# Four inverse roots per pair of tiles from GpSimd to VectorE, the share transposes inside their own pair, scatters unpaced

## The chip, the cores and the metric

One core of a Trainium2 chip runs the whole program. The metric is the device time of one launch in microseconds (us). The engines are TensorE (PE for matmuls, PEld for its weight loads), VectorE (DVE), ScalarE (ACT), GpSimd (POOL) and SyncE (SP, which starts plain DMAs). They run their own instruction streams in order and meet at semaphores.

## The reference, cut to what matters

Two layers of a graph transformer over 12500 nodes of 256 features. The change touches one stage only, the end of layer 0, which computes for each node:

```
xn = layernorm(x)
h  = sum over edges of weighted (xn @ W), + b               # the edge sums come from an earlier stage
h  = relu(0.5*((h-mu)*rsqrt(var+eps)*gamma + beta) + 0.5*xn)            # LN_H
m  = softmax_heads(xn @ Wq) @ context @ Wout;  m = (m-mu)*rsqrt(var+eps)*mix_gamma   # LN_MIX
x1 = x + h + m
t  = (x1-mu)*rsqrt(var+eps)                                             # LN_X1, the tokens
x2 = x1 + t + sum over 8 experts e of comb[e]*(gelu(t@w1[e]+b1[e])@w2[e] + b2[e])
     # comb: softmax shares of the two best experts of t @ router
y  = (x2-mu)*rsqrt(var+eps)                                             # LN_X2, for layer 1
```

Layer 1's keys and key-value context are gathered from y on the way. On the side, the stage scatters the 212500 edge records, three words each, into sorted order for layer 1.

## The kernel before

The stage is `finish_layer0`. It takes the nodes two tiles of 125 at a time (a pair, index j inside it), 50 pairs. It is software pipelined: the body `run(i)` does three pairs at once, the `front` of pair f = i+1 (everything up to tokens and shares), the experts (`moe`) of pair i and the `back` (LN_X2, y, keys, context) of pair i-1. Two bodies stand in a hardware loop of 24 turns (`pipeline`, Fori), the first and last bodies stand outside.

Each engine writes its body as 32 hand-numbered slots, and the order of the code is the order of execution. A slot holds one chunk of expert work, `up` (both tiles, half of the hidden features, product with w1) or `down` (one tile, product with w2): slots 0 and 1 are up(0,0), up(0,1), and from slot 2 each expert e takes four slots, up(e+1,0), up(e+1,1), down(e,0), down(e,1); the last four slots are down(6,0), down(6,1), down(7,0), down(7,1). Between the chunks TensorE does the front's and back's small products. What goes with each chunk on the other engines is `gelu` on ScalarE after an up and `expert_sum` on VectorE after a down (acc += comb*ps_dn). PSUM has two banks for up, two for down, one bank `ps_T` for transposes and one bank `ps_M` for all small products; every use of ps_T or ps_M waits until the last one was copied out.

What the change and the prediction name:

- `second_bias(j)` (TensorE L1915) is the product of the turned shares combT with b2, into ps_M; `add_b2(j)` (VectorE L1551) adds it to acc. Before, they stand in slots 0 and 1 (TensorE) and 1 and 2 (VectorE), ahead of expert 0's sum. second_bias(1) waits for add_b2(0), since both use ps_M.
- `turn_gates(j)` (TensorE L2018) turns the shares; before, in slots 30 and 31, in the body before the one that uses them, so it waits for `combine` (VectorE L1701, L1706) at once. `keep_gates(j)` (ScalarE L1834) copies the result out.
- `x_and_sums(j)` (VectorE L1577, L1581, slots 0 and 1) makes xn and the sums that `turn_xs(j)` (TensorE L1925, slots 2 and 3) turns.
- `statistics` (VectorE L1525, L1529) makes mean and variance of two tiles. `rstd` on GpSimd (L1457 add eps, L1460 power -0.5) turns variance into the inverse root of one of the four norms; VectorE then waits for it in `back_rows` (L1563, slot 3), `gcn_residual` (L1619, slot 13), `mixer_residual` (L1644, slot 20) and `tokens` (L1658, slot 23).
- `turn_tokens(j)` (TensorE L1951, slots 24 and 25) waits for tokens; `router(j)` (slots 26 and 27); `keep_logits`, `two_best` (VectorE L1670 to L1678, slot 27), `best_places`, `shares`, `combine` (slot 28).
- GpSimd's body is four rstd with 34 scatters of records (L1475) between them, in portions of 8, 6, 3 and 17: the inverse root of LN_X2 stands behind 17 scatters of the body before. At its end it waits for the scatters of the body before and gives their record buffer back (`share_done`), on which SP's load of the next records waits.

## Time and profile before

| | us |
|---|---|
| median of 3 runs | 9652.04 |
| lowest, highest | 9631.42, 9655.69 |
| the profiled execution | 9654.26 |
| its span in the trace | 9652.6 |

The stage runs from about 3124 to 5936 us of the span, its loop from about 3250 to 5850. In the section of rows below, "idle before, releaser" says how long an engine was idle ahead of an instruction and what ended that. A row `L1896 ... x4` of the time line is one up chunk and `L1904 ... x4` one down chunk: the program has two matmuls for it and the trace four records.

### The profile page before, as it was taken

Reading aid. Unit: us, or ns where it says so; the run is one execution under the profiler, and the core shown is the slowest. Engines: PE = TensorE matmul, PEld = TensorE weight load, DVE = VectorE, ACT = ScalarE, POOL = GpSimd, SP = SyncE. Lnnn points to the kernel's source line nnn. Section 1 sums busy time; section 2 is a strip of 40 time slices with the busy share of each in tenths; the row PEclk is TensorE's granted clock in tenths of the full one; section 3 lists DMA queues with packets and bytes.
Section 4 is the critical chain, followed back from the end, with each engine's and each line's share of the span. In section 5 each row is a group of like instructions: output and inputs, shape, how many; then the busy total and the mean of one; then the engine's idle time right before and its main releaser. Section 6 shows DMA issues by size and latency. Waiting matters only on the chain. (4 is left out here: it accounts for less than half of the span.)

```text
span 9652.6 us, 138544 instructions
## 1 busy us (share of the span) xinstructions
PE 7460.8 (77%) x34023; PEld 5523.6 (57%) x34023; DVE 5942.2 (62%) x19421; ACT 1695.4 (18%) x3225; POOL 5895.1 (61%) x6435
## 2 busy tenths in 40 slices
PE   4835767767676788888888886888888888877779
PEld 3623555555555566666666664555565555655556
DVE  5746777777777455555555554666666666657742
ACT  0000000000000333434344441111111111112210
POOL 3225777777776577777777776777777777730002
PEclk7657888888888899999999897898898898889989
DMA  1024333333333100000000001333333333323335
GB/s 50 31 74 125 109 108 107 109 107 109 107 109 105 28 17 17 16 16 17 17 17 16 16 18 39 106 104 100 107 103 102 105 103 103 105 84 92 94 95 167
DMA packets 464053, 737.22 MB, mean 76 GB/s; under 512 B 145169, under 2 KB 317487, under 8 KB 463067
## 3 DMA queue, kind: packets, MB, share of 16 engines
q0 software_dynamic: 235408, 493.09, 18.0%
q1 hardware_dynamic: 214944, 224.70, 8.1%
q10 hardware_dynamic: 13240, 15.44, 0.6%
q14 instruction: 435, 3.56, 0.1%
q8 instruction: 26, 0.43, 0.0%
HBM read 624.32 MB, written 108.50 MB: 76 GB/s over the span
## 5 line engine op out<-in xcount | busy, mean ns | idle before, releaser
L894 POOL DMA_INDIRECT sum_gathered<-table,sum_idx x3600 | 3505.0, 974 | 1238.9 <-issue 994.7
L959 PE MATMUL sum_agg_res<-sum_gathered,sum_lay 125*125 125x256 f32 x7200 | 2259.3, 454 | 982.9 <-DMA sum_gathered<-table,sum_idx 388.7
L959 PEld LDWEIGHTS sum_agg_res<-sum_gathered,sum_lay 125*125 125x125 f32 x7200 | 1473.5, 219 | 1530.1 <-DVE all_sums L944 941.2
L944 DVE TENSOR_TENSOR all_sums<-all_sums,sum_agg_res 125x256 f32 x3600 | 1508.6, 419 | 1016.0 <-PE sum_agg_res L959 846.1
L1475 POOL DMA_INDIRECT sorted_recs<-fin_rec,fin_pos x1700 | 1759.6, 1035 | 497.6 <-issue 490.3
L925 DVE TENSOR_SCALAR sum_lay<-all_lane,sum_dloc_now,sum_w_now 125x125 f32<-125x125 f32 x3612 | 1283.6, 356 | 21.0 <-DVE sum_xn_tiles L1076 17.2
L1896 PE MATMUL fin_ps_up<-fin_tokens_T,fin_w 128*128 128x250 f32 x3200 | 935.9, 426 | 0.0
L1904 PE MATMUL fin_ps_dn<-fin_w,fin_hidden 128*125 128x256 f32 x3200 | 817.6, 389 | 20.5 <-DVE fin_acc L1544 20.5
L1896 PEld LDWEIGHTS fin_ps_up<-fin_tokens_T,fin_w 128*128 128x128 f32 x3200 | 657.2, 218 | 140.4 <-issue 41.8
L1544 DVE SCALAR_TENSOR_TENSOR fin_acc<-fin_ps_dn,fin_comb,fin_acc 125x256 f32<-125x256 f32 x800 | 380.3, 481 | 511.9 <-PE fin_ps_dn L1904 509.1
L1904 PEld LDWEIGHTS fin_ps_dn<-fin_w,fin_hidden 128*125 128x125 f32 x3200 | 579.1, 190 | 127.4 <-issue 55.3
L1771 ACT ACTIVATE fin_hidden<-fin_ps_up,fin_b 128x250 f32<-128x250 f32 x800 | 375.6, 470 | 992.7 <-PE fin_ps_up L1896 989.3
L2673 POOL TENSOR_SCALAR slices_var_eps<-slices_mean_var 125x2 f32<-125x2 f32 x50 | 11.0, 219 | 615.5 <-DVE slices_mean_var L2716 603.6
L2425 PE MATMUL sum_ps_A<-sum_w,sum_low 128*125 128x256 f32 x1600 | 378.0, 379 | 0.0
L2416 PE MATMUL sum_ps_C<-sum_x_T,sum_w 128*128 128x500 f32 x800 | 368.4, 582 | 0.0
L2425 PEld LDWEIGHTS sum_ps_A<-sum_w,sum_low 128*125 128x125 f32 x1600 | 300.2, 188 | 116.0 <-issue 80.7
L1059 DVE CUSTOM_DVE_ANT_0 sum_junk<-sum_src_hot,sum_ps_rank 125x100 f32<-125x100 bf16 x1700 | 334.5, 251 | 2.2 <-PE sum_ps_rank L1127 2.2
L2790 PE MATMUL slices_ps_acc<-slices_xn,slices_sw 125*128 125x257 f32 x800 | 229.9, 439 | 121.2 <-DVE slices_sw L2741 121.2
L1049 DVE TENSOR_TENSOR sum_src_hot<-sum_lane,steps_src_tile 125x400 bf16<-125x400 bf16 x425 | 243.2, 572 | 69.9 <-PE sum_ps_rank L1135 62.5
L2348 ACT ACTIVATE sum_low<-sum_ps_C,sum_b 128x500 f32<-128x500 f32 x200 | 135.4, 677 | 721.9 <-PE sum_ps_C L2416 721.9
L2790 PEld LDWEIGHTS slices_ps_acc<-slices_xn,slices_sw 125*128 125x128 f32 x800 | 165.9, 218 | 166.6 <-DVE slices_sw L2741 142.2
L1111 ACT ACTIVATE sum_exp_key<-sum_key_less_max 125x256 f32<-125x256 f32 x100 | 41.6, 416 | 1249.3 <-DVE sum_key_less_max L1086 1249.3
(483 smaller groups left out, 10632.1 us busy)
## 6 DMA issues: line engine op xcount, KB each, us to landing
sum_gathered<-table,sum_idx POOLq DMA_INDIRECT x3600
sorted_recs<-fin_rec,fin_pos POOLq DMA_INDIRECT x1700, 2.1
slice_weights<-slices_sw SPq DMA_DIRECT2D x50, 480.0 KB
out_sw<-slice_weights SPq DMA_DIRECT2D x50, 480.0 KB
deg_x_tiles<-in_x SPq DMA_DIRECT2D x100, 125.0 KB
sum_x_tiles<-in_x SPq DMA_DIRECT2D x100, 125.0 KB
fin_x<-in_x SPq DMA_DIRECT2D x100, 125.0 KB
x<-fin_acc SPq DMA_DIRECT2D x100, 125.0 KB
```

Source lines behind the costliest of these rows:

```text
L894: eng.indirect_dma_start(out=self.rows[:, s % self.RING, :], out_offset=None, in_=self.table, in_offset=bass.IndirectOffsetOnAxis(ap=self. ...
L925: ins = eng.tensor_scalar(self.lay[:, g % 2, l, :], k.lane[0:P, 0:P], self.dl[:, s:s + 1], self.wl[:, s:s + 1], ALU.is_equal, ALU.mult)
L944: eng.tensor_tensor(sums, sums, res, ALU.add).then_inc(self.added, 1)
L959: eng.matmul(self.res[s % self.RES][:, 0, :], self.lay[:, g % 2, l, :], self.rows[0:P, s % self.RING, :], start=True, stop=True).then_inc( ...
L1475: eng.indirect_dma_start(out=k.sorted_recs, out_offset=bass.IndirectOffsetOnAxis(ap=pos[:, n, r:r + 1], axis=0), in_=rec[:, n, r, :], in_o ...
L1544: eng.scalar_tensor_tensor(out=acc[:, n, j, :], in0=ps_dn[j][:, :], scalar=comb[:, n, j, e:e + 1], in1=acc[:, n, j, :], op0=ALU.mult, op1= ...
L1771: eng.activation(hid[:, e % 2, c, :], ps_up[c][:, :], ACT.Gelu, bias=b1[:, c, e:e + 1])\
L1896: mm = eng.matmul(ps_up[c][:, :], w1[:, e, m, c * H2:(c + 1) * H2], xtT[:, n, m, :, :], start=(m == 0), stop=(m == 1))
L1904: mm = eng.matmul(ps_dn[j][:, :], hid[:, e % 2, m, j * P:(j + 1) * P], w2[:, e, m, :], start=(m == 0), stop=(m == 1))
L2416: mm = eng.matmul(ps_C[u % 2][:, 0:T], w1[:, m, u * 128:(u + 1) * 128], xT[:, m, :], start=(m == 0), stop=(m == 1))
L2425: mm = eng.matmul(ps_A[j // 2][0:P, (j % 2) * D:(j % 2 + 1) * D], hid[:, u % 2, j * P:(j + 1) * P], w2[:, u, :], start=(u == 0 and j % 2 = ...
L2790: mm = eng.matmul(ps_acc[c][:, :], sw[:, n, j, c * 128:(c + 1) * 128], xn[:, n, j, :], start=False, stop=False, skip_group_check=True)
```

## The change

Everything is in `finish_layer0`.

1. GpSimd's `rstd` and its constant `neg_half` go. VectorE gets `inverse_root(which, pair, first, last)`, twelve steps on a 125x2 tile, each waiting for the one before: add eps, shift the bits right by one, subtract from a constant (as integers), and three rounds of three steps each. The steps stand in groups of four: LN_X2 in slots 0 to 2, LN_H in 8 to 10, LN_MIX in 17 to 19, LN_X1 in 20 to 22.
2. `gcn_residual` is split: `gcn_scale` (slot 10) does (h-mean)*half_gamma in one instruction a tile and doesn't need the root; of five steps a tile at slot 13 three are left. `mixer_residual` likewise: `mixer_scale` in slot 18, and one step of three is left at slot 20.
3. `turn_gates` moves to slots 19 and 20 of the body that uses the shares, `keep_gates` on ScalarE to slots 20 and 21, `second_bias` to 21 and 23, `add_b2` on VectorE to 22 and 24. The banks' waits follow (up(0,0) to turn_xs(0) now have no small product ahead).
4. `turn_tokens` moves one slot on (25, 26), `router` to 27 and 28, its copies on ScalarE too; on VectorE keep_logits and two_best to 28, best_places 29, shares 30, combine 31.
5. GpSimd issues its 34 scatters in a row, and gives the record buffer of the body before back after the ninth.

```
+            def inverse_root(which, pair, first, last):
+                v, y, r = ve[:, which, :], root[:, which, :], rs[:, which, :]
+                for step in range(first, last):
+                    if step == 0:
+                        eng.wait_ge(mv_ready[which], pair + 1)
+                        eng.nop(nofuse=True)
+                        ins = eng.tensor_scalar(v, mv[:, which, :, 1], LN_EPS, None, ALU.add)
+                    else:
+                        eng.wait_ge(rs_steps[which], pair * 11 + step)
+                        if step == 1:
+                            ins = eng.tensor_scalar(y.bitcast(I32), v.bitcast(I32), 1, None, ALU.logical_shift_right)
+                        elif step == 2:
+                            ins = eng.tensor_scalar(r.bitcast(I32), y.bitcast(I32), -1.0, ROOT_SEED, ALU.mult, ALU.add)
+                        elif step % 3 == 0:
+                            ins = eng.scalar_tensor_tensor(out=y, in0=r, scalar=-0.5, in1=r, op0=ALU.mult, op1=ALU.mult)
+                        elif step % 3 == 1:
+                            ins = eng.tensor_tensor(y, y, v, ALU.mult)
+                        else:
+                            ins = eng.scalar_tensor_tensor(out=r, in0=y, scalar=1.5, in1=r, op0=ALU.add, op1=ALU.mult)
+                    ins.then_inc(rs_ready[which] if step == 11 else rs_steps[which], 1)
...
             def run(i, n, turn, front=True, moe=True, back=True):
...
-                if back:
-                    rstd(LN_X2, b)
-                scatter(0)
...
+                for r in range(RPP):
+                    eng.indirect_dma_start(
+                        out=k.sorted_recs, out_offset=bass.IndirectOffsetOnAxis(ap=pos[:, n, r:r + 1], axis=0),
+                        in_=rec[:, n, r, :], in_offset=None).then_inc(scattered[n], 16)
+                    if r == RPP // 4 and (not isinstance(i, int) or i > 0):
+
+                        eng.wait_ge(scattered[1 - n], (turn + n) * (16 * RPP))
+                        eng.sem_inc(S.share_done, 1)
...
                     if moe:
-                        if slot == 1 or slot == 2:
-                            add_b2(slot - 1)
+                        if slot == 22 or slot == 24:
+                            add_b2(slot // 2 - 11)
```

VectorE from the last chunk ahead of the mixer's norm to tokens (slots 20 to 24). Before:

```order
L1539 REGISTER_ALU
L1544 SCALAR_TENSOR_TENSOR fin_acc<-fin_ps_dn,fin_comb,fin_acc 125x256 [waits fin0_dn_kept,fin0_dn_done]
L1644 TENSOR_SCALAR fin_mix<-fin_mix,fin_mean_var,fin_rstds 125x256 [waits plan0_edges_in3]
L1644 TENSOR_SCALAR fin_mix<-fin_mix,fin_mean_var,fin_rstds 125x256
L1647 TENSOR_TENSOR fin_mix<-fin_mix,fin_mix_gamma 125x256 [waits fin0_m_chain] x2
L1649 TENSOR_TENSOR fin_acc<-fin_acc,fin_mix 125x256 [waits fin0_m_chain] x2
L1525 BN_STATS fin_stats<-fin_acc 125x6 [waits fin0_m_chain] x2
L1529 BN_AGGR fin_mean_var<-fin_stats 125x2 [waits rec_rec_src]
```

After, the same stretch from LN_X1's statistics on (L1539 is expert_sum, L1546 is add_b2, L1510 to L1522 the root):

```order
L1500 BN_AGGR fin_mean_var<-fin_stats 125x2
L1510 TENSOR_SCALAR fin_var_eps<-fin_mean_var 125x2 [waits rec_rec_consts]
L1514 TENSOR_SCALAR fin_roots<-fin_var_eps 125x2 [waits plan0_edges_in0]
L1516 TENSOR_SCALAR fin_rstds<-fin_roots 125x2 [waits plan0_edges_in0]
L1518 SCALAR_TENSOR_TENSOR fin_roots<-fin_rstds 125x2 [waits plan0_edges_in0]
L1532 REGISTER_ALU
L1539 SCALAR_TENSOR_TENSOR fin_acc<-fin_ps_dn,fin_comb,fin_acc 125x256 [waits fin0_dn_kept,fin0_dn_done]
L1520 TENSOR_TENSOR fin_roots<-fin_roots,fin_var_eps 125x2 [waits plan0_edges_in0]
L1522 SCALAR_TENSOR_TENSOR fin_rstds<-fin_roots,fin_rstds 125x2 [waits plan0_edges_in0]
L1518 SCALAR_TENSOR_TENSOR fin_roots<-fin_rstds 125x2 [waits plan0_edges_in0]
L1520 TENSOR_TENSOR fin_roots<-fin_roots,fin_var_eps 125x2 [waits plan0_edges_in0]
L1546 TENSOR_TENSOR fin_acc<-fin_acc,fin_ps_M 125x256 [waits fin0_dn_kept]
```

Eight root steps and one expert_sum now stand between the statistics and add_b2(0), which itself came from slot 1.

TensorE at slots 19 to 23, after (L2051 is turn_gates, L1912 up, L1920 down, L1933 second_bias); before, only the up and down rows stood here:

```order
L2051 MATMUL fin_ps_T<-all_ident,fin_comb 8x125 [waits fin0_comb_ready]
L1910 REGISTER_ALU
L1912 MATMUL fin_ps_up<-fin_tokens_T,fin_w 128x250 [waits fin0_up_kept]
L1912 MATMUL fin_ps_up<-fin_tokens_T,fin_w 128x250
L2051 MATMUL fin_ps_T<-all_ident,fin_comb 8x125 [waits fin0_comb_ready,fin0_cT_kept]
L1920 MATMUL fin_ps_dn<-fin_w,fin_hidden 125x256 [waits fin0_dn_kept,fin0_up_kept]
L1920 MATMUL fin_ps_dn<-fin_w,fin_hidden 125x256
L1933 MATMUL fin_ps_M<-fin_b,fin_comb_T 125x256 [waits fin0_cT_kept,fin0_mix_kept]
```

The four small products came here; the fourth, second_bias(1), stands two chunks further on, ahead of up(6,1), and waits for add_b2(0).

TensorE at the start of a body. Before (L1915 is second_bias):

```order
L1915 MATMUL fin_ps_M<-fin_b,fin_comb_T 125x256 [waits fin0_cT_kept]
L1894 ISA [waits fin0_xT_kept]
L1896 MATMUL fin_ps_up<-fin_tokens_T,fin_w 128x250 [waits fin0_up_kept]
L1896 MATMUL fin_ps_up<-fin_tokens_T,fin_w 128x250
L1915 MATMUL fin_ps_M<-fin_b,fin_comb_T 125x256 [waits fin0_cT_kept,fin0_acc_ready]
```

After (L1943 is turn_xs(0)):

```order
L1910 ISA [waits fin0_xT_kept]
L1912 MATMUL fin_ps_up<-fin_tokens_T,fin_w 128x250 [waits fin0_up_kept]
L1912 MATMUL fin_ps_up<-fin_tokens_T,fin_w 128x250
L1910 REGISTER_ALU [waits fin0_xT_kept]
L1912 MATMUL fin_ps_up<-fin_tokens_T,fin_w 128x250 [waits fin0_up_kept]
L1912 MATMUL fin_ps_up<-fin_tokens_T,fin_w 128x250
L1910 REGISTER_ALU
L1912 MATMUL fin_ps_up<-fin_tokens_T,fin_w 128x250 [waits fin0_up_kept]
L1912 MATMUL fin_ps_up<-fin_tokens_T,fin_w 128x250
L1941 ISA [waits fin0_xT_kept]
L1943 MATMUL fin_ps_T<-all_ident,fin_xn 128x125 [waits fin0_xs_ready]
```

Three up chunks now follow one another, and the next wait on VectorE is turn_xs(0)'s.

## Rows read from the trace of the kernel before

**Rows 1.** Windows, the loop: busy us and instructions by engine, clock, DMA share.

```profile
3250.00:5850.00 2600.00, 2276.28 (x9806) 1763.96 (x9804) 1369.02 (x4417) 1059.12 (x2049) 1854.91 (x1994) 0.91 0.07 17
```

**Rows 2.** Waits of TensorE in the loop: us in total, times, longest us.

```profile
PE fin_ps_M L1915 <- DVE fin_acc L1551: 120.6, 47, 4.7
PE fin_ps_T L1951 <- DVE fin_tokens L1658: 91.7, 47, 2.0
PE fin_ps_M L1931 <- DVE fin_gcn L1588: 49.3, 18, 4.5
PE fin_ps_T L2018 <- DVE fin_comb L1706: 34.3, 47, 0.7
PE fin_ps_dn L1904 <- DVE fin_acc L1544: 16.0, 47, 0.4
PE fin_ps_M L1931 <- DVE fin_query L1598: 7.8, 38, 0.2
```

**Rows 3.** Time line of TensorE: start us, us, instruction, idle before and its releaser.

```profile
4502.05 1.21 PE L1915 MATMUL fin_ps_M<-fin_b,fin_comb_T 8*125 8x256 f32 x2 [1.52 <-DVE fin_acc L1551]
4503.19 3.70 PE L1896 MATMUL fin_ps_up<-fin_tokens_T,fin_w 128*128 128x250 f32 x8
...
4532.64 1.01 PE L1896 MATMUL fin_ps_up<-fin_tokens_T,fin_w 128*128 128x250 f32 x4
4533.49 1.03 PE L2001 MATMUL fin_ps_ctx<-fin_next_norm,fin_krelu 125*128 125x257 f32 x4
...
4558.42 1.21 PE L1915 MATMUL fin_ps_M<-fin_b,fin_comb_T 8*125 8x256 f32 x2 [4.24 <-DVE fin_acc L1551]
```

**Rows 4.** Time line of ScalarE: a share copy, then the body's start.

```profile
4550.99 0.25 ACT L1834 COPY fin_comb_T<-fin_ps_T 8x125 f32<-8x125 f32 x1 [2.08 <-PE fin_ps_T L2018]
...
4554.28 1.28 ACT L1771 ACT_TABLE_LOAD   x1 [1.48 <-PE fin_ps_up L1896]
4555.57 0.47 ACT L1771 ACTIVATE fin_hidden<-fin_ps_up,fin_b 128x250 f32<-128x250 f32 x1
```

**Rows 5.** Time line of VectorE: shares and combine, then the body's start.

```profile
4549.13 0.15 DVE L1691 TENSOR_SCALAR fin_gate<-fin_gate 125x2 f32<-125x2 f32 x1
...
4549.52 0.16 DVE L1695 TENSOR_TENSOR fin_gate<-fin_gate 125x2 f32<-125x2 f32 x1
4549.60 0.88 DVE L1701 TENSOR_SCALAR fin_pick<-all_lane,fin_top_f,fin_gate 125x8 f32<-125x8 f32 x4
...
4550.68 0.88 DVE L1544 SCALAR_TENSOR_TENSOR fin_acc<-fin_ps_dn,fin_comb,fin_acc 125x256 f32<-125x256 f32 x2
...
4555.60 0.75 DVE L1525 BATCH_NORM_STATS2 fin_stats<-fin_acc 125x6 f32<-125x256 f32 x2 [2.68 <-issue]
...
4557.55 0.48 DVE L1581 SCALAR_TENSOR_TENSOR fin_sum_self<-fin_xn,all_dinv,all_sums 125x256 f32<-125x256 f32 x1 [0.18 <-DVE fin_xn L1577]
```

**Rows 6.** Waits of VectorE in the loop: us in total, times, longest us.

```profile
DVE fin_next_norm L1563 <- POOL fin_rstds L1460: 290.9, 47, 8.8
DVE fin_stats L1525 <- issue: 62.5, 23, 3.2
```

**Rows 7.** Time line of VectorE, mixer_residual's end and LN_X1's statistics.

```profile
4537.99 0.75 DVE L1649 TENSOR_TENSOR fin_acc<-fin_acc,fin_mix 125x256 f32<-125x256 f32 x2
...
4539.51 0.25 DVE L1529 BATCH_NORM_AGGREGATE fin_mean_var<-fin_stats 125x2 f32<-125x6 f32 x2
```

**Rows 8.** Time line of VectorE, the last pair's y.

```profile
5905.84 0.25 DVE L1529 BATCH_NORM_AGGREGATE fin_mean_var<-fin_stats 125x2 f32<-125x6 f32 x2
5918.70 0.74 DVE L1563 TENSOR_SCALAR fin_next_norm<-fin_acc,fin_mean_var,fin_rstds 125x256 f32<-125x256 f32 x2 [12.61 <-POOL fin_rstds L1460]
```

**Rows 9.** Groups by line in the loop: count, busy us, mean ns, idle before.

```profile
L1475 POOL DMA_INDIRECT sorted_recs<-fin_rec,fin_pos x1614 | 1672.9, 1037 | 472.1 <-issue 465.7 <-DVE fin_mean_var L1529 6.4
...
L1622 DVE TENSOR_TENSOR fin_gcn<-fin_gcn,fin_half_gamma 125x256 f32<-125x256 f32 x96 | 36.0, 415 | 0.0
```

**Rows 10.** Time line of GpSimd beside gcn_residual's first steps.

```profile
4528.18 3.75 POOL L1475 DMA_INDIRECT sorted_recs<-fin_rec,fin_pos  x1 [0.30 <-issue]
```

More of the change, by code:

```diff
@@ L1337, in finish_layer0 @@
         rs = sb("rstds", [P, 4, TE])
+        root = sb("roots", [P, 4, TE])
         rec = sb("rec", [LANES, 2, RPP, 3], I32)
@@ L1346, in finish_layer0 @@
         LN_X2, LN_H, LN_MIX, LN_X1 = range(4)
+        ROOT_SEED = 1597463007.0
+        B2_AFTER = 4
         w_in = sem("w_in")
@@ L1448, in _, with run @@
                          channel_multiplier=1).then_inc(spare_lanes, 1)
-            eng.memset(neg_half[:], -0.5).then_inc(S.power_ready, 1)
-            eng.wait_ge(S.power_ready, 1)
             eng.sem_inc(S.share_done, 1)
-            def rstd(which, pair):
-                eng.wait_ge(mv_ready[which], pair + 1)
+            def run(i, n, turn, front=True, moe=True, back=True):
+                if not moe:
+                    return
+                eng.wait_ge(rec_in[n], turn * 32 + 32)
@@ L1456, in rstd @@
                 eng.nop(nofuse=True)
-                eng.tensor_scalar(ve[:, which, :], mv[:, which, :, 1], LN_EPS, None, ALU.add).then_inc(rs_steps[which], 1)
-                eng.wait_ge(rs_steps[which], pair + 1)
-                eng.nop(nofuse=True)
-                eng.tensor_tensor(rs[:, which, :], ve[:, which, :], neg_half[:], ALU.pow).then_inc(rs_ready[which], 1)
-            def run(i, n, turn, front=True, moe=True, back=True):
-                f, b = (i + 1 if moe else i), i - 1
-                shares = [0, RPP // 4, RPP * 5 // 12, RPP // 2, RPP]
-                def scatter(part):
-                    if not moe:
-                        return
-                    if part == 0:
-                        eng.wait_ge(rec_in[n], turn * 32 + 32)
-                        eng.nop(nofuse=True)
-                    for r in range(shares[part], shares[part + 1]):
-                        eng.indirect_dma_start(
-                            out=k.sorted_recs, out_offset=bass.IndirectOffsetOnAxis(ap=pos[:, n, r:r + 1], axis=0),
-                            in_=rec[:, n, r, :], in_offset=None).then_inc(scattered[n], 16)
-                if back:
-                    rstd(LN_X2, b)
-                scatter(0)
-                if front:
-                    rstd(LN_H, f)
-                scatter(1)
-                if front:
-                    rstd(LN_MIX, f)
-                scatter(2)
-                if front:
-                    rstd(LN_X1, f)
-                scatter(3)
-                if moe and (not isinstance(i, int) or i > 0):
-                    eng.wait_ge(scattered[1 - n], (turn + n) * (16 * RPP))
-                    eng.sem_inc(S.share_done, 1)
@@ L1718, in run @@
                             back_norm()
+                        if slot < 3:
+                            inverse_root(LN_X2, b, slot * 4, slot * 4 + 4)
                         elif slot == 3:
@@ L1724, in run @@
                     if front:
+                        if 8 <= slot < 11:
+                            inverse_root(LN_H, f, slot * 4 - 32, slot * 4 - 28)
                         if slot < 2:
@@ L1734, in run @@
                             query_softmax(slot - 8)
+                        elif slot == 10:
+                            gcn_scale()
                         elif slot == 13:
@@ L1840, in run @@
                             gelu(e, c)
+                        if slot == 20 or slot == 21:
+                            keep_gates(slot - 20)
                     if front:
@@ L2044, in run @@
                             mixer(slot - 15)
-                        elif slot == 24 or slot == 25:
-                            turn_tokens(slot - 24)
-                        elif slot == 26 or slot == 27:
-                            router(slot - 26)
-                        elif slot == 30 or slot == 31:
-                            turn_gates(slot - 30)
+                        elif slot == 25 or slot == 26:
+                            turn_tokens(slot - 25)
+                        elif slot == 27 or slot == 28:
+                            router(slot - 27)
             pipeline(eng, run)
```

143 lines of the change are left out of this document (87 added, 56 removed).

## The prediction, made before the changed kernel ran

> **What bounds the kernel now.** The page averages over stages with different limits, and the change is in one of them, so the first view is the window of that stage's loop. It [rows 1] says that TensorE is busy 2276 of 2600 us, 88%, and no other engine over 71%: TensorE sets the pace, and what counts is its idle time and its clock. 2600 us hold 47.6 pairs, so a pair takes 54.6 us, of which TensorE idles 6.8.
>
> Next come TensorE's waits in the loop [rows 2]. The six sums make 319.7 us, 6.8 us for each of 47 pairs, so nothing is missing. The reader is to see that all of them end with VectorE, and where: at second_bias(1) for add_b2(0) (120.6 us, 2.57 a pair), at turn_tokens for tokens (91.7, 1.95), at query(0) for gcn(0) (49.3, in 18 pairs only, 1.05 on average), at turn_gates for combine (34.3, 0.73) and behind it at down(7,1) (16.0, 0.34). VectorE's own waits [rows 6] say why query(0) waits: back_rows stands ahead of gcn(0) and waits for GpSimd's LN_X2 root, 6.2 us a pair (290.9 over 47), as that root is queued behind 17 scatters.
>
> Then the clock. The granted clock of the loop is 0.91 of 2.4 GHz [rows 1]; with two levels, 2.4 and 1.2, it stood at 1.2 GHz for 18% of the time, 9.8 us a pair. The time line [rows 3] shows that it falls behind the waits: after the 1.52 us wait two up chunks take 3.70 us, where one takes 0.85 start to start at full clock (4532.64 to 4533.49). With some of that time idle, about 4.3 us a pair are lost. Work at full clock is then 54.6 - 6.8 - 4.3 = 43.5 us a pair, and the change leaves it as it is: no matmul is added or removed.
>
> **The change, part by part.** Each part is priced as TensorE's wait in one pair.
>
> *Waits that go.* With add_b2, turn_gates and second_bias out of slots 30 to 2, and the LN_X2 root on VectorE, the first, third, fourth and fifth row of [rows 2] go: 2.57 + 1.05 + 0.73 + 0.34 = 4.69 us. turn_tokens' 1.95 goes too, if tokens are early enough in slot 25 (below). Together 6.64. The 7.8 us at query(1)'s bank stay.
>
> *A root step on VectorE.* The nearest rows are the three dependent steps of shares on 125x2 tiles [rows 5]: 4549.13 to 4549.52 is two of them, 0.195 us a step. I take 0.2. Below, a step can't cost less than the 0.15 that such an instruction is busy, above I allow 0.25 for the register instruction ahead of each. One root is 2.4 us, four are 9.6 us a pair; 1.3 us go with the fused scale steps. VectorE has 1369 of 2600 us busy [rows 1], so it has room; only the roots that stand on a chain to TensorE cost: four steps ahead of x_and_sums(0), eight ahead of add_b2(0). LN_H's and LN_MIX's first eight steps lie beside TensorE's work in slots 8 to 19; without that cover LN_MIX's would cost 1.6.
>
> *New wait A, start of a body.* TensorE now has three up chunks, 3 x 0.85 = 2.55 us, before turn_xs(0), counted from the end of down(7,1). VectorE reaches the last expert_sum 0.35 us after that point (result 0.15, shares' steps 0.2), needs 0.40 for it and 1.1 for combine, which now stands here (4549.52 to 4550.68 with one step of shares, [rows 5]); then statistics to the end of the first sum_self, 4555.60 to 4557.55 + 0.48 = 2.43; then four root steps in between, 0.8. xs is ready at 5.1: a wait of 2.55. Part of it is taken earlier: up(1,0) needs gelu(0,0), which comes 1.28 + 0.47 us behind its up [rows 4], so 1.3 us of the wait stand there and cost nothing more. Every second body has VectorE's 2.7 us at the loop's back edge (62.5 over 23) [rows 6], now with nothing less behind it: a wait of 5.2. Mean 3.85 us. turn_xs(1) is 1.8 behind turn_xs(0) on VectorE and 1.3 on TensorE, but after such a wait TensorE runs at half clock, so I count nothing.
>
> *New wait B, turn_gates(1).* ps_T must be copied out first, and keep_gates(0) stands behind gelu(5,1) on ScalarE, hence behind up(5,1): from the point where TensorE could go on, 0.16 for the result (a chunk's 1.01 less 0.85 [rows 3]), 0.47 for the gelu and 0.25 for the copy [rows 4], with the handshakes 0.9 us. Queued behind it on TensorE are down(4,0) and all of the following; VectorE waits for that down too, so wait C isn't shortened.
>
> *New wait C, second_bias(1).* It waits for add_b2(0). On VectorE from the result of down(4,0) on: expert_sum 0.40 (two take 0.88, one 0.48 [rows 5]), mixer_residual's last step to the end of the statistics 4537.99 to 4539.76, 1.77 [rows 7], a first root group 0.8, expert_sum(4,1) 0.40, a second group 0.8, add_b2 0.42, handshakes 0.15: 4.75. TensorE has in that time second_bias(0) 0.6 (1.21 at half clock [rows 3]), down(4,1) 0.87 (as the context's 1.03 less 0.16), up(6,0) 0.85, less the 0.17 by which the result came later: 2.17. The wait is 2.6 us. Tokens follow 1.3 us after add_b2(0) and TensorE needs 3.2 to turn_tokens, so that wait is gone.
>
> *New wait D, router(1).* It needs keep_logits(0), which in slot 28 stands behind expert_sum(6,0), and that behind down(6,0): 0.17 for the result, 0.40, 0.17 for a small instruction, 0.05 for the handshake: 0.8 us.
>
> *Scatters.* Nobody on TensorE's path waits for them. 34 of 1.037 + 0.30 us [rows 9] are 45.5 us a pair, under 54.6; the early share_done frees SP, which waits for y_ready anyway. Cost nothing; if a pair came under 45.5 us they would be the bound.
>
> *Ends.* The last pair's y waits 12.6 us for GpSimd [rows 8]; 2.5 us of steps take its place: -10 us once. The first pair's roots lie bare: +2.
>
> *Sum.* New waits 3.85 + 0.9 + 2.6 + 0.8 = 8.15, old ones 6.64: +1.5 us a pair. The loss to the clock I leave at 4.3: as many long waits (A and C for the b2 and the tokens wait), each a little longer. 49 pairs with experts: 49 x 1.5 - 8 = +66 us on the profiled execution's 9654.3: **9720 us**, 0.7% over it and over the median, 9652.0, which lies 2 us below. With steps of 0.15 or 0.25 us (twelve of them count) it is 9690 or 9750; the clock's loss may be 0.8 us a pair off either way, 40 us.
>
> **The rivals.**
>
> *The clock stays up (faster).* Now the small stalls in slots 26 to 2 come close together, [rows 2] first, fourth and fifth. After the change wait A is one place, and between B and C lie 3.4 us of work. If only one fall of the clock a pair is left, the loss halves to 2.1: -108 us against the forecast, 9612. It decides from a loss under 3 us a pair on (low clock under 7 us). Against it: C is longer than the 1.52 us wait after which the clock fell.
>
> *Steps are nearly free (no change).* Independent small instructions start much closer than dependent ones; if a root step cost 0.1 us, A and C would shrink by 0.4 and 0.8, the wait sum would be 6.95, and 49 x 0.3 - 8 = +7 gives 9661. Against it: the shares' steps, the same shape with the same kind of wait.
>
> *Scatters and VectorE block each other (slower still).* The time line shows a scatter of 3.75 us [rows 10] beside gcn_residual's first two-input instructions, while those stay at 415 ns [rows 9]: GpSimd gives way, VectorE never. The Trainium skill, SBUF — State Buffer, section "SBUF: two separate sides", says that whichever of the two starts first holds the shared ports for its whole instruction and the other fully blocks. By that rule unpaced scatters would also stop VectorE's two-input root steps; this trace shows it one-sided only. In this kernel it would be half a scatter, 0.5 us, in each of the three root groups on a chain: 49 x 1.5 = +73 over the forecast, 9793.
>
> **How the numbers follow.** The forecast's case has 0.50 (9720, own range 9680 to 9770); clock 0.22 (9612); free steps 0.20 (9661); blocked 0.08 (9793). The range goes from 9600 to 9800: it leaves out some of the clock's case and the upper half of the blocked one. A measurement can tell 0.3%, 29 us, from no change. Faster is the clock's case, 0.22; the same is the free steps' case, 0.20; slower the rest, 0.58.
>
> **What would show it.** In TensorE's waits of the loop: second_bias(1) on add_b2 some 2.6 us a pair, turn_gates(1) on keep_gates 0.9, router(1) on keep_logits 0.8, turn_xs(0) some 2.5 and 5.2 in turn less what stands at up(1,0), and no row for tokens or for gcn. Root steps 0.2 us start to start. GpSimd's scatters ahead of the experts, back_rows without a wait. The forecast is wrong if the waits sum to 7 us a pair or less, or if the granted clock of the loop leaves 0.91 by more than 0.02: at 0.95 the loop alone would give 2 us a pair.

## The result and the profile after

The kernel after takes 9662.6 us (median of 11 runs, 9655.3 to 9672.2) against 9638.5 for the kernel before (11 runs, 9631.3 to 9655.7): 1.0022 times, interval 1.0014 to 1.0031. That is 24 us where 66 were forecast, inside the range, but within the 0.3% that the prediction calls no change, to which it gave 0.20.

TensorE's window over the same stretch as [rows 1] (PE, PEld, DVE, ACT, POOL busy, granted clock, DMA share, GB/s), and TensorE's waits there, which answer to [rows 2]:

```profile
3250.00:5850.00 2600.00, 2217.45 (x9534) 1703.05 (x9533) 1660.63 (x6329) 1015.55 (x1995) 1526.30 (x1575) 0.93 0.07 16
```

```profile
PE fin_ps_T L1943 <- DVE fin_sum_self L1576: 148.0, 68, 5.2
PE fin_ps_M L1933 <- DVE fin_acc L1546: 107.9, 46, 2.4
PE fin_ps_up L1912 <- ACT fin_hidden L1787: 49.3, 46, 1.1
PE fin_ps_T L2051 <- ACT fin_comb_T L1850: 32.0, 46, 0.7
PE fin_ps_M L1949 <- DVE fin_logit L1669: 29.9, 46, 0.7
PE fin_ps_M L1949 <- DVE fin_query L1593: 9.5, 46, 0.2
```

All waits of the kernel before but query(1)'s are gone, and the four foreseen ones stand in their places: A in the first and third row (turn_xs, and its part at up(1,0)), C in the second, B in the fourth, D in the fifth. Over 46 pairs, A is 4.29 us, C 2.35, B 0.70 and D 0.65. The time line shows wait C (2.28 us), and the slower matmuls behind it: eight of down take 3.17 us where four took 1.09 before it; the granted clock is 1.00 up to 4511.6 us, 0.68 to 4513 and 0.50 to 4515.

```profile
4504.19 1.09 PE L1920 MATMUL fin_ps_dn<-fin_w,fin_hidden 128*125 128x256 f32 x4
4510.09 0.69 PE L1933 MATMUL fin_ps_M<-fin_b,fin_comb_T 8*125 8x256 f32 x2 [2.28 <-DVE fin_acc L1546]
4511.66 3.17 PE L1920 MATMUL fin_ps_dn<-fin_w,fin_hidden 128*125 128x256 f32 x8
```

VectorE's root steps, from the same time line, beside one of GpSimd's unpaced scatters (the first row) start 0.20 us apart. The last row is the group of one such step in 3250 to 5850 us (busy, mean ns, idle time before):

```profile
4508.99 0.96 POOL L1459 DMA_INDIRECT sorted_recs<-fin_rec,fin_pos  x1 [0.30 <-issue]
4509.12 0.16 DVE L1522 SCALAR_TENSOR_TENSOR fin_rstds<-fin_roots,fin_rstds 125x2 f32<-125x2 f32 x1
4509.32 0.16 DVE L1518 SCALAR_TENSOR_TENSOR fin_roots<-fin_rstds 125x2 f32<-125x2 f32 x1
4509.52 0.16 DVE L1520 TENSOR_TENSOR fin_roots<-fin_roots,fin_var_eps 125x2 f32<-125x2 f32 x1
```

```profile
L1520 DVE TENSOR_TENSOR fin_roots<-fin_roots,fin_var_eps 125x2 f32<-125x2 f32 x554 | 88.1, 159 | 14.4
```

The surprise is outside the changed stage. From the first to the last instruction of each stage, in us; the second column is a second trace of the kernel before:

| stage | before | before, traced again | after |
|---|---|---|---|
| first layer's sums | 2332 | 2328 | 2326 |
| first layer's experts (the change) | 2811 | 2806 | 2862 |
| second layer's sums, untouched | 2556 | 2549 | 2525 |
| slices, untouched | 704 | 704 | 704 |

The experts' stage is 51 us longer than in the first trace (56 than in the second), but the second layer's sum stage, whose code and data the change doesn't touch, is 30 us shorter (24). With the first layer's sums, 6 us shorter, that makes 15 of the 16 us by which the two profiled executions differ. GpSimd gathers rows through both sum stages. The group of its gathers on the page (busy, mean ns, then GpSimd's idle time ahead of them) is first of before, then of after: 42 us less idle. The group takes in both layers; 576 us of the idle time stand in the first layer in either kernel, so all of the difference lies in the second.

```profile
L894 POOL DMA_INDIRECT sum_gathered<-table,sum_idx x3600 | 3505.0, 974 | 1238.9 <-issue 994.7
```

```profile
L894 POOL DMA_INDIRECT sum_gathered<-table,sum_idx x3600 | 3502.2, 973 | 1197.3 <-issue 999.8
```

VectorE's time line at the top of the second layer's loop shows what differs. The first block is one turn of before, the second one of after; the idle time in brackets is put down to "issue", with nothing waited for. Over the whole stage such idle time of VectorE ahead of these three lines is 223 us before and 187 after:

```profile
6439.72 0.20 DVE L914 CAST sum_dloc_now<-steps_dloc_p 125x78 f32 x1 [3.45 <-issue]
6442.26 0.21 DVE L915 COPY sum_w_now<-steps_w_p 125x78 f32 x1 [2.33 <-issue]
6443.81 0.42 DVE L944 TENSOR_TENSOR all_sums<-all_sums,sum_agg_res 125x256 f32 x1 [0.87 <-issue]
```

```profile
6479.80 0.28 DVE L914 CAST sum_dloc_now<-steps_dloc_p 125x78 f32 x1 [2.83 <-issue]
6479.92 0.20 DVE L915 COPY sum_w_now<-steps_w_p 125x78 f32 x1
6483.33 0.42 DVE L944 TENSOR_TENSOR all_sums<-all_sums,sum_agg_res 125x256 f32 x1 [2.71 <-issue]
```

GpSimd then waits for TensorE, and TensorE for VectorE's adds. This is GpSimd's longest wait of that turn, before and after:

```profile
6448.00 1.10 POOL L894 DMA_INDIRECT sum_gathered<-table,sum_idx  x1 [3.76 <-PE sum_agg_res L959]
```

```profile
6487.51 1.10 POOL L894 DMA_INDIRECT sum_gathered<-table,sum_idx  x1 [2.17 <-PE sum_agg_res L959]
```

And the queue that brings instructions moved 145 packets in this stage before (6040 to 8560 us) and 121 after (6088 to 8577 us; packets, MB, share), one less for each of the loop's 24 turns:

```profile
q14 instruction: 145, 1.19, 0.2%
```

```profile
q14 instruction: 121, 0.99, 0.1%
```

### The profile page after: what moved, and what is told of

The parts are those of the page before. It is cut to its first block and busy times, and to the rows that moved or that the text cites. A ratio compares the mean times of both kernels' runs of the same rounds, so it can differ in the third digit from the quotient of the medians.

```text
span 9668.8 us, 141279 instructions
## 1 busy us (share of the span) xinstructions
PE 7460.3 (77%) x34023; PEld 5504.9 (57%) x34023; DVE 6293.9 (65%) x21621; ACT 1679.3 (17%) x3225; POOL 5592.9 (58%) x6034
## 5 line engine op out<-in xcount | busy, mean ns | idle before, releaser
L894 POOL DMA_INDIRECT sum_gathered<-table,sum_idx x3600 | 3502.2, 973 | 1197.3 <-issue 999.8
L1459 POOL DMA_INDIRECT sorted_recs<-fin_rec,fin_pos x1700 | 1651.5, 971 | 1166.8 <-DMA fin_pos<-pos_d 663.4
L1912 PE MATMUL fin_ps_up<-fin_tokens_T,fin_w 128*128 128x250 f32 x3200 | 862.8, 397 | 51.4 <-ACT fin_hidden L1787 51.4
L1920 PE MATMUL fin_ps_dn<-fin_w,fin_hidden 128*125 128x256 f32 x3200 | 901.8, 420 | 0.2 <-DVE fin_acc L1539 0.2
L1539 DVE SCALAR_TENSOR_TENSOR fin_acc<-fin_ps_dn,fin_comb,fin_acc 125x256 f32<-125x256 f32 x800 | 386.0, 483 | 591.9 <-PE fin_ps_dn L1920 583.2
L1920 PEld LDWEIGHTS fin_ps_dn<-fin_w,fin_hidden 128*125 128x125 f32 x3200 | 628.6, 206 | 134.0 <-issue 42.1
L1912 PEld LDWEIGHTS fin_ps_up<-fin_tokens_T,fin_w 128*128 128x128 f32 x3200 | 600.6, 201 | 173.5 <-ACT fin_hidden L1787 86.6
```

The lines of the kernel that those rows point to most:

```text
L894: eng.indirect_dma_start(out=self.rows[:, s % self.RING, :], out_offset=None, in_=self.table, in_offset=bass.IndirectOffsetOnAxis(ap=self. ...
L1459: eng.indirect_dma_start(out=k.sorted_recs, out_offset=bass.IndirectOffsetOnAxis(ap=pos[:, n, r:r + 1], axis=0), in_=rec[:, n, r, :], in_o ...
L1539: eng.scalar_tensor_tensor(out=acc[:, n, j, :], in0=ps_dn[j][:, :], scalar=comb[:, n, j, e:e + 1], in1=acc[:, n, j, :], op0=ALU.mult, op1= ...
L1912: mm = eng.matmul(ps_up[c][:, :], w1[:, e, m, c * H2:(c + 1) * H2], xtT[:, n, m, :, :], start=(m == 0), stop=(m == 1))
L1920: mm = eng.matmul(ps_dn[j][:, :], hid[:, e % 2, m, j * P:(j + 1) * P], w2[:, e, m, :], start=(m == 0), stop=(m == 1))
```

## The experiments

Each ratio is to the kernel before, run beside it on the same chip. The first eight kernels ran on two chips on which before takes 9641 and 9645 us. "Place" is how many instructions further on VectorE's loop of the second layer's sum stage stands than in before, in the built program; in the kernel after it is 251.

### Where a loop stands

```
+        spare = sb("spare", [P, 5])
...
             eng.wait_ge(w_in, 12 * 16)
+            for c in range(5):
+                eng.memset(spare[:, c:c + 1], 0.0)
```

> The kernel after, with five memsets of one spare column each at the head of VectorE's program for the second layer's sum stage: about 0.3 us of work that nothing waits for, but all of VectorE's later instructions stand five places further on, in the count of the built program 256 places behind the kernel before instead of 251. Theory P (the kernel after gained in this later stage only because its longer VectorE program puts the stage's loop where one fetch of instructions less is needed a turn: 145 packets of the instruction queue fell to 121 over the 24 turns, and about 51 us of VectorE's idle time at L915 went): the packets go back to about 145, the stage to about 2546 us from its 2516, and the whole to 1.0053 times the kernel before, some 30 us over the kernel after's 1.0022. Rival Q (the gain comes from the records, the scatters or the gathers, that is from data and DMA and not from where the code lies): no change, 1.0022, packets at 121 or whatever, stage at 2516.

Measured: 1.0054 (1.0042 to 1.0066), 144 packets, the stage 2542 us: 17 longer than in the kernel after, where 30 were expected. The same with 16 memsets in the kernel before:

> The kernel before, with sixteen such memsets at the same place: the first layer's experts are untouched, and VectorE's loop of the later stage stands 16 places further on. Theory P: the packets of the instruction queue in that stage fall from 145 to about 121, VectorE's idle time at L915 (51.3 us, 24 times) goes, and the whole takes about 30 us less, 0.997 times the kernel before. Rival Q: no change, 1.000.

Measured: 0.9927 (0.9914 to 0.9939), 122 packets. Theory P holds in direction and packets, but its size was off: 70 us for this kernel, not 30. The stage is 2465 us long; the turn below has one long stall at the top instead of two, and no wait of GpSimd over 1 us behind it:

```profile
6415.54 0.40 DVE L914 CAST sum_dloc_now<-steps_dloc_p 125x78 f32 x1 [3.04 <-issue]
6415.66 0.32 DVE L915 COPY sum_w_now<-steps_w_p 125x78 f32 x1
6417.31 0.42 DVE L944 TENSOR_TENSOR all_sums<-all_sums,sum_agg_res 125x256 f32 x1 [0.84 <-issue]
```

Theory P (only where the loop lies against the fetches counts, and the experts' stage has no part in it): that stage takes about 2465 us as with 16 memsets, not 2525, the packets of the instruction queue in it are 121 or 122, and the whole is 60 us under the kernel after: 1.0022 - 0.0062 = 0.996. Rival Q (the 70 us of the run with 16 memsets belong to something else in the kernel before, as its spread-out scatters): 1.002.

Measured: 0.9967 (0.9953 to 0.998), the stage 2474 us, 121 packets. GpSimd's group on the pages of these three runs, in the order 5 memsets in after, 16 in before, 21 in after:

```profile
L894 POOL DMA_INDIRECT sum_gathered<-table,sum_idx x3600 | 3497.7, 972 | 1237.2 <-issue 988.1
```

```profile
L894 POOL DMA_INDIRECT sum_gathered<-table,sum_idx x3600 | 3493.0, 970 | 1162.7 <-issue 991.5
```

```profile
L894 POOL DMA_INDIRECT sum_gathered<-table,sum_idx x3600 | 3492.3, 970 | 1160.4 <-issue 993.3
```

Places 0 and 256 give 1238.9 and 1237.2 us of idle time, 16 and 272 give 1162.7 and 1160.4, whichever kernel is around them; 251, and -5 in the kernel with b2 alone below, give 1197.3 and 1200.2. Places that are equal modulo 256 give equal idle time to 3 us. The stages agree less well: 2556, 2549 and 2542 us at places 0, 0 and 256, 2465 and 2474 at 16 and 272, 2525 and 2529 at 251 and -5. So GpSimd's 42 us of idle time less in the kernel after come from the place of VectorE's loop. The memsets change nothing else, so no data or scatters are needed to explain it; of the stage's 24 to 30 us, 17 come back with five memsets, and the rest is within the 14 us by which stages at one place differ.

### Each half of the change alone

First roots, scale steps and scatters alone, with the rest as in before; its edit against the kernel after, on VectorE, cut, takes add_b2 back to slots 1 and 2:

```
                     if e == 0:
-                        eng.wait_ge(S.xt_added, i * TE + j + 1)
-                    elif e == B2_AFTER + 1:
                         eng.wait_ge(S.acc_ready, i * TE + j + 1)
...
-                        if slot == 22 or slot == 24:
-                            add_b2(slot // 2 - 11)
+                        if slot == 1 or slot == 2:
+                            add_b2(slot - 1)
```

Then the kernel before with gates, b2 and the router's steps alone moved.

> The kernel before with the change's first two parts alone: roots on VectorE with the fused scale steps, unpaced scatters, share_done at the ninth; turn_gates, second_bias, add_b2 and the router's steps stay in slots 30 to 2 and 1 to 28 as in the kernel before. VectorE's later loop stands 257 places on, one past a whole number of fetches, so it keeps the stage of before (2555 us). Theory W (each root step costs 0.2 us where it stands on a chain to TensorE): query(0)'s wait of 1.05 us a pair goes, second_bias(1)'s grows by the first group of LN_X2's root, 0.8 us, turn_tokens' stays between 1.5 and 2.4: the experts' stage within 25 us of before's 2811, ratio 0.998 to 1.003. Rival R (the roots alone cost what the kernel after lost): stage at 2860, ratio 1.005.

> The kernel before with the change's third part alone: gates, second_bias and add_b2 in slots 19 to 25, router and combine one to three slots later; the roots stay on GpSimd between the paced scatters. Theory W: without root groups on the chains, second_bias(1) waits 2.35 - 1.6 = 0.75 us and turn_xs(0) about 0.8 less than in the kernel after (4.3 down to 3.5), turn_gates 0.7 and router 0.65 stay, query(0)'s 1.05 for GpSimd's LN_X2 root stays: 6.6 us a pair as before, and the experts' stage within 30 us of before's 2811; with the later stage's 30 the ratio is 0.994 to 1.000. Rival B (moving gates and b2 is what costs the kernel after its 50 us): stage at 2860, ratio 1.002.

Measured: 1.0043 (1.0026 to 1.0059) and 1.0067 (1.005 to 1.0085), the experts' stage 2873 and 2913 us. Theory W missed both: the first came out near rival R (2860 us, 1.005), the second well past rival B (2860 us, 1.002). The two losses, 62 and 102 us, don't add up to the change's 51. TensorE's waits in 3250 to 5650 us, of the roots alone (43 pairs):

```profile
PE fin_ps_M L1927 <- DVE fin_acc L1544: 168.0, 42, 6.1
PE fin_ps_T L1963 <- DVE fin_tokens L1655: 117.9, 43, 2.8
PE fin_ps_T L2030 <- DVE fin_comb L1703: 33.1, 42, 1.1
```

and of b2 alone (42 pairs), with VectorE's wait for GpSimd's LN_X2 root:

```profile
PE fin_ps_M L1938 <- DVE fin_gcn L1591: 111.1, 21, 5.4
PE fin_ps_M L1922 <- DVE fin_acc L1554: 78.7, 42, 1.9
PE fin_ps_T L1932 <- DVE fin_sum_self L1584: 75.4, 42, 3.9
```

```profile
DVE fin_next_norm L1566 <- POOL fin_rstds L1461: 200.9, 42, 7.6
```

With the roots alone, second_bias(1) still stands at the start of the body, and add_b2(0) has a root group and, every second time, the loop's back edge (the jump back to its top) ahead of it: 3.9 us a pair where 3.4 were expected. Tokens cost 2.75 where at most 2.4 were expected, as LN_X1's twelve steps stand ahead of them. With b2 alone the wait at the start of the body is gone, but back_rows still waits for GpSimd's root, and together with the back edge it holds gcn(0): 5.3 us in every second pair, 2.6 a pair where 1.05 were expected. Each half removes what the other leaves as the next to be late: the roots take away back_rows' wait, b2's move takes add_b2 out of the back edge's reach. That account fits the rows but is argued, not shown: the run meant to test its first half (roots_late, below) fell where it could not. Nor does any run move VectorE's loop of the experts' stage alone. Its "issue" idle time in 3250 to 5850 us grew by 17 us in three rows (fin_stats 62.5 to 69.2, fin_xn 11.2 to 13.4, fin_acc of expert_sum 0 to 7.9), so a part of the 51 us may be that.

### The new waits one by one

x_and_sums(0) ahead of back_norm and the first root group:

```
+                    if front and slot < 2:
+                        x_and_sums(slot)
                     if back:
                         if slot == 0:
                             back_norm()
```

> The kernel after, with x_and_sums(0) and (1) written ahead of back_norm and of the first root group in slots 0 and 1, the same number of instructions. Theory W (TensorE's wait at turn_xs(0) is VectorE's queue ahead of x_and_sums(0): combine 1.1 us, statistics 1.15, four root steps 0.8, and every other time the loop's back edge): statistics and root group no longer stand ahead, so the wait on sum_self falls from 3.2 us a pair (148 us over 46) to about 1.3, and the one at up(1,0) partly: 1.5 to 1.9 us a pair less, 75 to 95 us over 49 pairs, 0.993 to 0.995 times the kernel before. Rival V (the time is set by VectorE's whole chain and the wait only moves): what goes at turn_xs comes back at gcn, query or turn_y, and the time stays within 20 us of the kernel after, 1.0022.

add_b2(0) ahead of LN_X1's second root group:

```
-                        if slot == 22 or slot == 24:
-                            add_b2(slot // 2 - 11)
+                        if slot == 24:
+                            add_b2(1)
                         kind, e, c = chunk(slot)
                         if kind == "down":
                             expert_sum(e, c)
+                        if slot == 21:
+                            add_b2(0)
```

> The kernel after, with add_b2(0) on VectorE right behind expert_sum(4,1) and ahead of the second group of LN_X1's root steps instead of behind it. Theory W (root steps cost 0.2 us each where they stand on the chain to second_bias(1)): that wait falls by four steps, 0.8 us, from 2.35 to 1.55 us a pair, -39 us, and tokens, later by nothing, stay ahead of turn_tokens: 0.998 times the kernel before. Rival T (tokens come next): turn_tokens begins to wait for tokens by what second_bias(1) no longer waits, and the time stays at 1.0022.

Measured: 0.9924 (0.9912 to 0.9936) and 0.9931 (0.9919 to 0.9943); the experts' stage 2757 and 2771 us, 105 and 91 under the kernel after. TensorE's rows for the moved waits, in 3250 to 5650 us, first of x_first, then of b2_early:

```profile
PE fin_ps_T L1943 <- DVE fin_sum_self L1576: 94.6, 66, 3.3
```

```profile
PE fin_ps_M L1935 <- DVE fin_acc L1546: 73.6, 44, 1.7
```

Wait A at turn_xs is 2.1 us a pair instead of 3.2, C 1.66 instead of 2.35: the second as expected to 0.1 us, the first fell 0.8 less than expected. The gain is more than the waits. A pair takes 53.8 and 54.2 us, of which TensorE waits 7.1 and 7.3; the kernel after takes 56.0 with 8.1. So 1.1 and 0.8 us of wait gone brought 2.2 and 1.9 us. The clock can account for the rest. The windows of the kernel after, of x_first and of b2_early:

```profile
3250.00:5650.00 2400.00, 2046.62 (x8790) 1571.21 (x8789) 1530.72 (x5842) 933.25 (x1836) 1409.99 (x1455) 0.92 0.07 16
```

```profile
3250.00:5650.00 2400.00, 2079.78 (x9153) 1598.12 (x9152) 1592.49 (x6084) 974.86 (x1917) 1466.84 (x1513) 0.95 0.08 17
```

```profile
3250.00:5650.00 2400.00, 2068.89 (x9094) 1600.54 (x9094) 1579.79 (x6039) 969.96 (x1903) 1459.34 (x1506) 0.94 0.08 17
```

With two levels, 0.92, 0.95 and 0.94 put TensorE at 1.2 GHz for 9.0, 5.4 and 6.5 us of a pair. Half of the difference, 1.8 and 1.2 us, is an estimate of what the clock gives back, and 1.1 are to be explained in either kernel.

### A version with all four waits attacked

x_and_sums of both tiles first, combine in the next body, mixer_residual in slot 19, add_b2(0) behind the first root group in slot 20, turn_gates(1) in slot 21, keep_logits(0) ahead of expert_sum(6,0). Two things are added that belong to none of the four waits: 18 memsets, which put the later loop at place 272, and on ScalarE a one-element Gelu behind the router's exp, so that its table is loaded before gelu(0,0). The Gelu's edit, cut:

```
+                def load_gelu():
+                    if inner or i > 0:
+                        eng.wait_ge(warmed, i)
+                    eng.activation(warm[:], b1[0:1, 0, 0:1], ACT.Gelu).then_inc(warmed, 1)
...
                             exp_router()
+                            if moe:
+                                load_gelu()
```

> The kernel after with every new wait attacked: x_and_sums(0) and (1) first in slot 0 and combine in slot 1 of the next body (wait A), turn_gates(1) in slot 21 behind down(4,1)'s place (B), mixer_residual in slot 19 and add_b2(0) in slot 20 right behind LN_X1's first root group (C), keep_logits(0) ahead of expert_sum(6,0) (D), and one 1-element Gelu behind exp_router so that ScalarE's table is loaded before gelu(0,0) (the 1.07 us a pair at up(1,0)); and 18 memsets so that VectorE's later loop stands at place 272. Theory W with the clock: the waits fall from 8.2 to 1 to 3 us a pair, of which the back edge's every second pair is most, the low clock from 8.5 to under 4 us a pair: 47 to 49 us a pair, the experts' stage 2400 to 2550 us against 2861, and the later stage at 2465: ratio 0.945 to 0.962. Rival V (VectorE's or GpSimd's own chain sets the pace once the waits are moved, with 34 scatters of 0.97 + 0.3 us, 43 us a pair, and VectorE 35 us): TensorE's waits come back elsewhere and the stage stays over 2650, ratio over 0.97.

Measured: 0.9688 (0.967 to 0.9707), 9350 us, faster than both kernels. The sum stage is 2475 us, 10 over what was expected, and the memsets' part of the gain; it is 50 under the kernel after. The experts' stage is 2602, 260 under it, between the theories' numbers. TensorE still waits 4.8 us a pair.

```profile
PE fin_ps_M L1969 <- DVE fin_gcn L1586: 104.6, 47, 2.7
PE fin_ps_M L1953 <- DVE fin_acc L1549: 64.0, 47, 1.5
PE fin_ps_T L1963 <- DVE fin_sum_self L1579: 54.6, 23, 2.9
```

```profile
3250.00:5650.00 2400.00, 2164.39 (x9744) 1696.84 (x9743) 1676.75 (x6469) 1051.80 (x2085) 1579.49 (x1611) 0.96 0.08 18
```

B, D and the wait at up(1,0) are gone, C is 1.35 us a pair and the back edge's part of A is left, but query(0) now waits 2.2 us a pair for gcn(0), behind back_norm, combine and two root groups. So rival V was half right: of the waits taken away, part came back in another place.

### On slower chips

Nine more runs, of the kernel after and four others, fell on three other chips, on each of which the kernel before takes 11540 to 11635 us instead of 9640.

> The kernel after itself, as a control for the three that follow. All theories: 1.0022, within 0.2%, where the kernel before takes about 9640 us. On a chip where before takes 11570 us, theory K (that chip lengthens all waits between the engines of these two stages alike) gives within 2% of before, theory L (it strikes the kernels with the change more, as the four ratios of 1.05 to 1.08 suggest) 1.05 to 1.08.

> The kernel after with share_done given back behind the last scatter of a pair instead of behind the ninth. All theories: GpSimd waits 13 us a pair for the next records' places in the kernel after (613 us over 46 in the same scatters of the roots-only run), so the records come some 30 us later but before GpSimd is through; the prediction says this part costs nothing: 1.0022, within 0.2%. If the early share_done carried part of the result, as by records arriving too late, the ratio would go over 1.005.

> The roots-only kernel with LN_X2's three root groups moved from slots 0 to 2 to slots 4 to 6 and back_rows behind the last, so that no root step stands ahead of add_b2(0) any more. Theory G (the roots-only run lost its 61 us in the experts' stage because root groups stand on the chain to second_bias(1): 4.0 us a pair there against 2.57 in the kernel before, twice over with the clock): that wait falls to 2.6 to 3.2 us, query(0) waits no more than before, and the stage comes to 2780 to 2825 us from 2872, ratio 0.995 to 0.999 with the later stage as in the kernel before. Rival H (the loss comes from VectorE's longer program, its fetches, or from the tokens' later root): stage stays over 2850, ratio over 1.002.

> The combined kernel with the two waits it still had taken on: LN_X2's root and back_rows in slots 4 to 6 behind gcn and query (the 2.2 us a pair at query(0) for gcn(0)), and add_b2(0) directly behind expert_sum(4,0) with LN_X1's statistics and first root group behind it (the 1.4 at second_bias(1)); VectorE's later loop at place 272 again. Theory W with the clock: the waits fall from 4.8 to 1 to 2 us a pair (the loop's back edge is left), with the clock 4 to 6 us a pair less: the experts' stage 2300 to 2420 us against 2601, ratio 0.938 to 0.952. Rival V (VectorE's own chain sets the pace: its work is only moved): waits come up at turn_y, tokens or keep_logits instead, the stage stays over 2500, ratio over 0.958.

Measured there: the kernel after 1.0745 (1.0715 to 1.0775), so theory L. The late share_done came to 1.0738 and, on the chip of that control, to 1.0752 (1.0723 to 1.0782): it costs nothing there, as said. roots_late came to 1.0783, 1.0828 and 1.0777 in its three runs; since the kernel after loses as much there, they tell nothing of G and H. combined2 came to 1.0525, and to 1.0577 beside the control's 1.0745: faster than after, slower than before. combined2_64 came to 1.053, its sum stage 3019 us against 3036 in combined2. The same code on another of these chips took 3054, so P1 and P2 are open. Whether combined2 beats combined on the other chips is open too.

What differs there is when TensorE's results are seen. In the time line of the kernel after (after_again), the matmuls of down(6,0) end at 4150.9, and VectorE, which waits for nothing else, reads the result at 4178.0:

```profile
4149.76 1.11 PE L1920 MATMUL fin_ps_dn<-fin_w,fin_hidden 128*125 128x256 f32 x4
4178.01 0.48 DVE L1539 SCALAR_TENSOR_TENSOR fin_acc<-fin_ps_dn,fin_comb,fin_acc 125x256 f32<-125x256 f32 x1 [31.21 <-remote]
4178.62 1.00 PE L1949 MATMUL fin_ps_M<-fin_w_router,fin_tokens_T 128*125 128x8 f32 x4 [27.75 <-issue]
```

From 4155 to 4178 us no matmul is recorded and the granted clock is 0.50, while GpSimd issues its scatters at the usual 1.27 us. The ends of matmuls are modelled, so the trace doesn't tell whether TensorE was still at work. The wait comes back about once in every pair. TensorE's waits at its products into ps_M, the router's above all, in 4500 to 7900 us (38.6 pairs):

```profile
PE fin_ps_M L1949 <- issue: 570.8, 23, 29.2
PE fin_ps_M L1949 <- DVE fin_logit L1669: 457.9, 16, 30.9
```

These 26.7 us a pair are most of the 32 by which a pair is longer there. The experts' stage takes 4464 us instead of 2862, the first sums 3038 instead of 2326, the slices 706 instead of 704. Why the change costs 7% there could not be settled, since the trace of before came from another chip:

> The kernel before itself. On the chip where it takes 11600 us: the profile of after there has 3038 us in the first layer's sum stage, 4464 in the experts' stage and 3049 in the second layer's sum stage. Theory K1 (all 870 us between before and after lie in the experts' stage, where TensorE's results come late at the router each pair): before shows 3500 to 3650 us in that stage and the other two within 50 us of after's. Rival K2 (the difference is spread over all stages with matmuls): the sum stages are 150 us or more shorter too. On a chip where before takes 9640 us: 2331, 2811 and 2556 us, each within 15.

Measured: 0.9998 (0.9985 to 1.0011) on a chip where before takes 9637 us; stages of 2328, 2806 and 2549 us, 3 to 7 us from the first trace. That is how well a stage repeats, and neither K1 nor K2 was tested.

## Why the prediction was wrong, and where it was right

**Right: the bound and the waits.** The forecast had A 3.85, B 0.9, C 2.6, D 0.8, 8.15 in all; measured are 4.29, 0.70, 2.35, 0.65, together 7.98. The 6.64 us of old waits are gone. A pair grew from 54.6 to 56.0 us, by 1.4 where 1.5 were forecast. Most of A's excess stands at the back edge: turn_xs(0) waits 1.4 and 4.9 us in turn, with 1.07 at up(1,0) ahead, so 2.5 and 6.0 where 2.55 and 5.2 were forecast. A root step is 0.2 us, so "steps are nearly free" fell. Beside unpaced scatters root steps keep that spacing, and VectorE's two-input instructions are not held up (a step 159 ns, add_b2 416 before and after), so the rival by which scatters and VectorE block each other fell too. The Trainium skill, SBUF — State Buffer, section "SBUF: two separate sides", says of a VectorE instruction with two inputs in SBUF and a GpSimd instruction that reads SBUF that whichever starts first blocks the other. The traces show one direction of it, a scatter of 3.75 us beside two-input instructions [rows 10], and not the other.

**Right in size, by luck in part: the clock.** The loss was left at 4.3 us a pair. A pair less its waits is 47.9 us before and 47.9 after, so the sum of work and loss stayed, though the loop's granted clock went from 0.91 to 0.93, the edge of what the prediction allowed. How much of the 47.9 the clock took in each kernel isn't separated. The single-wait runs show that keeping the loss fixed was no law: where only one wait shrank, by about 1 us, a pair less its waits fell to 46.8, in the combined kernel to 45.8.

**A little off: the ends.** -8 us were counted; in the traces the first pair and everything behind the last turn_xs are 16 us shorter. With 48 intervals of 1.39 us that gives the stage's +51.

**Wrong: the sum's last step.** "49 x 1.5 - 8 = +66 us on the profiled execution" takes all other stages as unchanged: a term at nothing, without a reason given. The experts' +51 was a fair hit. The second layer's sum stage gave 24 to 30 us back, as VectorE's program got 251 instructions longer ahead of its loop; the first layer's sums gave 3 to 6, no more than a stage repeats by. The diff shows those instructions, and the trace of before shows both the instruction queue and VectorE's "issue" idle time at the top of that loop (81.4 and 51.3 us ahead of L914 and L915). The working used VectorE's back edge in the experts' loop [rows 6], but never asked where the other loops of that engine would come to stand. By the later runs that term can be anything from 0 to -91 us (the stage at places 0 and 16), which is enough to give "same" as much as "slower". The trace of before alone shows that such idle time exists, and not that it moves.

**Costs nothing, as said:** the early share_done, shown on the slower chips alone.

## What to carry to other kernels

When an edit changes the number of an engine's instructions, all its later loops move against the instruction fetches: count packets of the instruction queue and "issue" stalls by turn, and try a few dead instructions ahead of a hot loop before believing a per cent either way; here 16 memsets brought 70 us. Place a wait's cause away from a loop's back edge, and look at both halves of a change together, since each may hide the other's cost. Taking about 1 us of wait off TensorE brought about 2 in two kernels here, but that is no fixed price: the change added 1.3 us of wait a pair and cost 1.4, and the combined kernel took 3.3 away and gained 5.4. Compare stages, not only totals, and trace the unchanged kernel twice to know how well a stage repeats.

## What was not expected of the hardware

The stage around a loop of 391 VectorE instructions, with 24 turns, took 2465 to 2556 us, with 70 us of it shown in the whole program's time by moving the loop 16 places. In the turns shown, the stalls at the top were 3.45 + 2.33 us at place 0, 2.83 + 2.71 at 251 and 3.04 + 0.84 at 16, with the packets of the instruction queue at 145, 121 and 122 for the stage. And the same two kernels that stand at 1.0022 on one chip stand at 1.0745 on another, on which before itself takes 20% longer.
